# Layer 1 of a two-layer edge-convolution network on one core: GpSimd's two adds of a step ahead of its four gathers

## What is computed

```python
def _edge_conv(x, src, dst, W1, b1, W2, b2):
    x_i = x[dst]
    x_j = x[src]
    h = jnp.concatenate([x_i, x_j - x_i], axis=-1)
    m = _leaky(h @ W1 + b1) @ W2 + b2
    return jax.ops.segment_sum(m, dst, num_segments=N_NODES)

h = jnp.maximum(_layernorm(x, axis=-1), 0.0)
h = _edge_conv(h, src, dst, W1_0, b1_0, W2_0, b2_0)
h = _leaky(_layer_norm(h, ln_g0, ln_b0))
h = _edge_conv(h, src, dst, W1_1, b1_1, W2_1, b2_1)
h = _leaky(_layer_norm(h, ln_g1, ln_b1))
return x + h
```

## Time and profile before

| | |
|---|---|
| median of the runs shown | 1081.89 us |
| lowest and highest of them | 1065.54, 1090.26 us |
| the profiled execution | 1051.49 us, its span 1049.8 us |
| granted TensorE clock, mean | 0.938 |
| PE, DVE, ACT busy | 848.6, 816.5, 591.7 us |
| POOL busy | 727.7 us |
| POOL: gathers of layer 1 | 196, 197.4 us |
| POOL: adds (L597) | 98, 127.3 us |
| DVE: L856 of the form e_n <- e_v | 50, 59.3 us |

### The profile page before, as it was taken

One profiled execution on the slowest core, in us unless ns is written; L12 is line 12 of the kernel. 1 busy time (PEld: TensorE's weight loads), 2 busy tenths in 40 slices (PEclk: granted clock), 3 DMA queues, 4 the chain that ended last, 5 costly groups with the idle time before them and its releaser, 6 DMA issues.

```text
span 1049.8 us, 21951 instructions
## 1 busy us (share of the span) xinstructions
PE 848.6 (81%) x5756; PEld 691.8 (66%) x5756; DVE 816.5 (78%) x2330; ACT 591.7 (56%) x1632; POOL 727.7 (69%) x705
## 2 busy tenths in 40 slices
PE   1577788898889898988998647998888888888864
PEld 1345676777777677766777545777777777777753
DVE  6675687787887788787876313799999999999984
ACT  0145787888888788887888410433434343343431
POOL 4877777777777777777730007788888888888544
PEclk9998899999999999999999855999999999999965
DMA  1232477888687778776875551699999999999996
GB/s 38 77 81 76 109 173 190 210 201 212 182 211 190 203 193 214 193 203 179 199 183 133 145 151 49 149 246 276 272 272 265 270 270 259 276 267 266 256 265 174
DMA packets 338395, 204.11 MB, mean 194 GB/s; under 512 B 32986, under 2 KB 322589, under 8 KB 338269
## 3 DMA queue, kind: packets, MB, share of 16 engines
q1 hardware_dynamic: 190397, 99.95, 38.6%
q10 hardware_dynamic: 129056, 64.16, 22.2%
q0 software_dynamic: 18816, 38.57, 14.2%
HBM read 124.92 MB, written 77.62 MB: 193 GB/s over the span
## 4 chain that ended last, share of the span: by engine, by line
POOL 32%; DVE 23%; issue 21%; PE 8%; DMA 7%; ACT 4%; SPq 3%; DVEq 0%; ACTq 0%; POOLq 0%
POOL e_x L583 18%; POOL e_x L576 14%; DVE e_hT L856 5%; DVE e_n L856 5%; PE psum L902 3%; DVE e_same L750 3%; DMA e_x<-in_x,src_cols 3%; DVE e_rows L866 3%; DVE e_hidT L877 2%; SPq L531 2%; DMA b_rows<-e_rows 2%; DVE w_rel L735 1%; DMA h_rows<-w_out 1%; ACT e_n L633 1%; DVE n_stats L799 1%
## 5 line engine op out<-in xcount | busy, mean ns | idle before, releaser
L583 POOL DMA_INDIRECT e_x<-h_rows,src_cols x196 | 197.4, 1007 | 148.0 <-DMA h_rows<-w_out 93.9
L902 PE MATMUL psum<-w_win,w_oh 113*128 113x128 f32 x1568 | 227.0, 291 | 36.0 <-ACT w_out L613 21.7
L583 POOL DMA_INDIRECT e_x<-in_x,src_cols x196 | 205.9, 1051 | 59.8 <-issue 59.5
L576 POOL DMA_INDIRECT e_x<-in_x,dst_idx x196 | 194.2, 991 | 73.1 <-issue 58.2
L902 PEld LDWEIGHTS psum<-w_win,w_oh 113*128 113x128 f32 x1568 | 206.9, 205 | 42.2 <-issue 31.5
L618 ACT ACTIVATE e_v<-psum 128x512 f32<-128x512 f32 x98 | 59.4, 606 | 218.2 <-DVE e_hT L856 96.7
L910 PE MATMUL psum<-e_same,e_m 128*128 128x136 f32 (+2 forms) x1168 | 169.7, 290 | 0.0
L910 PEld LDWEIGHTS psum<-e_same,e_m 128*128 128x128 f32 x1168 | 149.3, 197 | 23.2 <-issue 21.2
L738 DVE TENSOR_TENSOR w_oh<-node_iota,w_rel 112x512 f32<-112x512 f32 x196 | 142.1, 725 | 6.7
L799 DVE BATCH_NORM_STATS2 n_stats<-e_x 128x6 f32<-128x128 f32 x392 | 80.4, 278 | 70.2 <-DMA e_x<-in_x,src_cols 69.1
L633 ACT ACTIVATE e_n<-e_x,n_shift,n_inv 128x128 f32<-128x128 f32 x196 | 80.5, 490 | 0.7 <-DVE n_shift L833 0.5
(11 more groups left out here) (164 smaller groups left out, 1677.9 us busy)
## 6 DMA issues: line engine op xcount, KB each, us to landing
w_win<-b_rows SPq DMA_DIRECT2D x784, 56.4 KB
h_rows<-w_out SPq DMA_DIRECT2D x98, 256.0 KB
e_line<-dst_lines SPq DMA_DIRECT2D x49, 288.0 KB
b_rows<-e_rows SPq DMA_DIRECT2D x49, 258.0 KB
b_rows<-e_rows ACTq DMA_DIRECT2D x49, 258.0 KB
e_x<-in_x ACTq DMA_DIRECT2D x49, 256.0 KB, 5.0
out<-e_x ACTq DMA_DIRECT2D x49, 256.0 KB
w_out<-in_x ACTq DMA_DIRECT2D x36, 256.0 KB, 4.8
```

The costliest lines, as they stand in the source:

```text
L576: pool.indirect_dma_start(e_x[:, slot, 0, k, :], None, table, bass.IndirectOffsetOnAxis(dst_idx[:, g * K + k:g * K + k + 1], 0)).then_inc( ...
L583: pool.indirect_dma_start(e_x[:, slot, 1, k, :], None, table, bass.IndirectOffsetOnAxis(src_cols[:, g * K + k:g * K + k + 1], 0)).then_inc ...
L902: last = nc.tensor.matmul(b_p[:, j, :], w_oh[0:W + 1, w % RH, j, :], w_win[0:W + 1, w % RW, j, 0:D], start=True, stop=True)
```

## The change

In layer 1 POOL takes the two adds of its step first and its four gathers after them. The waits of each stay with it. Layer 0 and all other engines have the same instructions in the same order.

```diff
             for s in range(-2, STEPS[1] + 1):
-                if active(s + 2):
-                    gather(pool, 1, s + 2)
                 for w in windows(s - R1 - 5):
                     pool.wait_ge(nodes_made, NODE_GROUPS + w + 1)
                     pool.wait_ge(x_in[w % RQ], 16 * uses(w, RQ) + loads_of(w) - 16)
                     pool.tensor_tensor(x_ring[w % RQ], t_ring[w % RT], x_ring[w % RQ], ALU.add).then_inc(nodes_raised, 1)
+                if active(s + 2):
+                    gather(pool, 1, s + 2)
```

## The result

The changed kernel took **1071.37 us** (median of 20 runs, 1056.30 to 1092.76). The kernel before, run beside it, took 1065.6 us (20 runs, 1044.74 to 1090.26). Ratio 1.0177, 95% interval 1.0141 to 1.0213. A ratio here compares only the executions within 1.5% of the fastest of their kernel (6 of the 20 before and 11 of the 20 after), so it need not be that of the medians, which lie 0.5% apart. The profiled execution took 1069.9 us with a span of 1068.2, against 1051.5 and 1049.8: the same ratio.

A forecast was written before the change was run, and what follows sets the result against it. GpSimd was taken to set layer 1's 7.65 us step; an earlier start with 8.21 us steps ends 21 us later, 1051.5 becoming 1072.6 profiled. The same 21 us on the runs' median of 1081.9 gives 1103 us, range 1074 to 1122.

The forecast's parts named there:

- the two locks: Layer 1: GpSimd's adds hold off VectorE's L856 by 1.42 us; VectorE's two-SBUF-input operations delay gathers by 0.2 to 0.3 us.
- The rule for late gathers: A gather starting during a two-SBUF-input VectorE operation is late by that operation's start + 0.57 − the gather's start.
- The start: Step 9 in layer 1: first adds at 687.17 instead of 692.15, beside L877, then holding off L882.
- rival A: Layer 1: L882 gets between the adds, VectorE is caught at L735 and L738; 7.89 us steps, +7 us, 1089; 25 in 100.
- My own pattern: Layer 1: adds hold off L882, three gathers are late, step 8.21 us instead of 7.65, 21 us later; 45 in 100.
- (a): Layer 1 gathers issued later against their use: costed at nothing, since even a landing of 6.0 us leaves 1.9.
- rival B: Layer 1: nothing happens, adds again meet L866 and L856 of the next step; 7.65 us, 1082; 8 in 100.
- (b): Layer 1: gather(s+2) queues behind the adds' wait for L856; costed at nothing, with 0.25 us to spare.
- (c): ACT's output stores issue up to 5 us sooner, SP's queue waits for nothing of POOL in layer 1; costed at nothing.
- the 30.4 us: Whole kernel: median of the three runs shown (1081.9) above the profiled execution (1051.5), carried into the forecast of 1103.
- The chances by size: Whole kernel: 35 in 100 for slower by over 2%, 61 for within 2%, 4 for faster by over 2%.

The follow-up runs named there:

- e5: The kernel before, unchanged, profiled again in another execution: 1047.63 us.
- e3: Changed order, with the first adds (step 9 only) waiting for both node blocks instead of one: 1075.58 us (4 runs), no ratio.
- e1: Changed order, with the first adds waiting once for VectorE's L862 of step 10: 1077.44 us (6 runs), ratio 1.0194.
- e11: Kernel before, with the first adds waiting once for L862 of step 10, repeated on another chip: 1057.24 us (12 runs), ratio 1.0017.
- e6: Kernel before, with the first adds waiting once for VectorE's L862 of step 10: 1045.90 us (10 runs), ratio 0.9928.
- e2: Kernel before, with the first adds waiting once for VectorE's L750 of step 10: 1075.78 us (12 runs), ratio 1.0011.
- e9: Kernel before, with the adds of every step from the fifth waiting for L862 of VectorE's next step: 1075.01 us (6 runs), ratio 1.0193.
- e10: Changed kernel, with the adds of every step from the fifth waiting for L862 of VectorE's next step: 1079.68 us (4 runs), ratio 1.0262.
- e7: Kernel before, with the second add of each step moved from GpSimd to VectorE behind L856: 1060.20 us (12 runs), ratio 1.0046.
- e8: Changed order, with the second add of each step moved from GpSimd to VectorE behind L856: 1060.98 us (12 runs), ratio 1.0071.
- e4: Kernel before, with GpSimd's adds cut to one element per partition: 1055.00 us (10 runs), ratio 0.9900.
- e12: Changed kernel, with GpSimd's adds cut to one element per partition: 1067.35 us (5 runs) beside 1067.43 for the kernel before, no ratio.

## Why the prediction was right or wrong

*The bound and the two locks: right.* GpSimd sets the step, VectorE's wait is the adds' hold-off. The rule for late gathers held in places that it had not been made from: the gather at 869.02 inside L738 of 868.93 should be late by 868.93 + 0.57 − 869.02 = 0.48 and is by 0.50 (1.44 − 0.94); the one at 872.02 inside L856 of 871.66 by 0.21, and is by 0.20. The Trainium skill, "SBUF — State Buffer", section "Who interferes with whom", has it that `tensor_tensor` does not stall GpSimd's descriptor generation; no stretch of the changed kernel has the 7.35 us step that would follow, and a gather of 1.44 against 0.94 speaks against it. But the gather also reads its indexes (`src_cols`) out of SBUF, and what is held off may be that read and not the descriptors: no run here tells the two apart.

*The start: the first step that failed.* I had the first adds at 687.17 beside L877. They began at 688.30, having waited 2.87 us for VectorE. GpSimd was done with its gathers by 685.43 (forecast 687.14), and VectorE's L856 pair stood at 687.53 instead of 685.64, after 0.89 us of waiting for a window at 685.41. The adds so met L856's second half and were held off, and L882 got in between them with 1.05 instead of 2.7. A start that was fixed to some tenths from one execution of another kernel was not to be had: e5 shows the kernel of before itself starting elsewhere, and by the table below L877 of step 9 moves over 25 us with TensorE's clock.

*The place: rival A's, not mine.* "L882 gets in between here too [...], DVE slips past and is caught later in its step, at L735 and L738", given 25 in 100, is what happened, for the reason given there: the first add had itself been held off. That isn't the only way: in e3 it wasn't, and L882 got in all the same. My own pattern is real and closes on itself (e1: 8.20, e5: 8.25), but it was not the one entered.

*The size in rival A: mis-sized.* It had 7.89 us a step, with "gather 1 behind L738 and one gather behind L856: 7.35 + 0.30 + 0.24". Measured: 7.35 + 0.50 + 0.20 = 8.05. I had put 0.30 for the first gather without laying the step out. L735 is held off until 866.86 + 1.82 = 868.68, so L738 starts at 868.93, only 0.09 ahead of the gather, and the rule gives 0.48. From VectorE's side: 6.24 + 1.82 = 8.06, where A had 1.65 of waiting. Hence 13.9 in the steps and not A's 9 − 2; with the 1.9 of the start that is 15.8 at L877 of step 48.

*What was costed at nothing.* The landing (a) was safe in the L735 place (866.34, the last issue's end, to L877 of the group at 872.86: 6.5 us) but not everywhere: 4.0 to 4.7 us in e1, against the 3.6 that the L856 place leaves. "The trace has no landing time for a gather under this load" was wrong: the packet records of the kernel before have the last packet 3.0 to 5.4 us behind the last issue, 4.0 in the median (groups 11 to 46). That spoke against rival B from the start, since its place leaves 3.6. That is why rival B (7.65, nothing happens) was closed to this order; I had looked at the landing in my own place only. The margin (b) played no part in the steady step, ACT's and SP's queues (c) neither.

*The sum.* Mine, +21 on 1051.5, gives 1072.6; the profiled execution took 1069.9, near it by other terms: 1.9 at the start, 13.9 in the steps, 2.6 in the tail, against 21 from 38 steps of 8.21. So that the forecast of 2.0% (1103 on 1081.9) lies next to the measured ratio of 1.0177 is in good part luck: the changed step gives 13.9 us, 1.3%. By the runs, 1103 was too high and 1071.37 lies 2.6 under the range's end. The failed term is the 30.4 us from the profiled execution to the median of three runs: beside the changed kernel the one before has a median of 1065.6, not 1081.9, 14.1 above its profiled execution. Three runs of a kernel that spreads over 45 us don't fix a median. The chances by size (within 2%: 61) fit the ratio of 1.0177, whose interval crosses 1.02.

*Where each profiled execution spent its time.* The 650 to 700 column is TensorE's granted clock just ahead of the first adds, where TensorE was busy for 46 to 50 of the 50 us; the next two are read at L877 (L879 or L881 in kernels with added lines).

| | clock, 650 to 700 | L877 of step 9 at, us | from there to step 48, us |
|---|---|---|---|
| e5, before again | 1.00 | 679.7 | 303.2 |
| e11, before, one wait | 0.97 | 684.2 | 300.9 |
| before | 0.94 | 686.8 | 299.1 |
| e6, before, one wait | 0.74 | 690.5 | 299.0 |
| e2, before, one wait | 0.83 | 692.1 | 320.4 |
| e3, changed, one wait | 0.97 | 688.8 | 313.2 |
| changed | 0.87 | 688.7 | 313.0 |
| e1, changed, one wait | 0.50 | 704.9 | 324.0 |
| e9, before, wait in every step | 0.50 | 703.5 | 315.3 |
| e10, changed, wait in every step | 0.90 | 685.8 | 327.6 |
| e7, before, split | 0.64 | 698.1 | 308.6 |
| e8, changed, split | 0.91 | 686.3 | 308.6 |
| e4, before, tiny adds | 0.97 | 683.9 | 301.1 |
| e12, changed, tiny adds | 0.69 | 697.5 | 292.6 |

The last column goes by place, by waits for gathers (e1, e10) and by single late results (e1, e2), not by that clock. The column before it spreads over 25 us with hardly an add run yet, and goes with the clock; the two executions at 0.50 are the latest.

*Cause.* Shown: the place sets the step (e2, e5), the two orders cost the same where one add forces both into one place (e7, e8), and the changed order doesn't stay in the 7.65 place from a start from which the order of before does (e1, e6), with L877 waiting for gathers (e1, e10). The lowest of 20 runs fits: 1056.3, where before reaches 1044.7. Open: how many executions of either kernel run in which place, since only the profiled ones can be seen. Of the old order three (before, e6, e11) kept 7.65 to 7.67 from the second adds on at the latest and two (e2, e5) had other steps as well; of the changed order two (changed, e3) had 8.06 and one (e1) ended at 8.20. Open too is what the change costs on average: the medians of 20 say 0.5%, the ratio 1.8%, and the table's 13.9 us 1.3%. And open is how much of the spread of all runs is TensorE's clock: in the profiled ones up to 25 us lie ahead of step 9, and its mean over an execution is 0.93 to 0.94 in the fastest runs of before and 0.89 to 0.92 in most of those over 1065 us.

## What to carry to other kernels

Where two engines that share an SBUF interface run in lock step, a change of order changes which instructions meet, and the step follows from that place: lay out the step for each place it can fall into, with every hold-off, and ask of each whether the data still land in time there. Look at more than one execution before building on the phase of one, and compare profiles between two marks inside the stretch, since what happened ahead of it can weigh more than the change. And a reordering that gains nothing in the sum of work can still cost the slack that the best place needs.

## What the runs showed that I had not expected

- A `tensor_scalar` on 112x4 numbers, one input in SBUF, is held off through both adds: 2.04 us instead of 0.22. The Trainium skill, "SBUF — State Buffer", section "Who interferes with whom", lists `tensor_scalar` among those that can take the shared pair; the trace agrees. Its rule that whoever issues first has the pair doesn't fit the steady step: L735 asks at 866.86, during the first add, and the second add passes it.
- One late result (0.91 us at L862, e5) moves the kernel from a step of 8.25 to one of 7.65 for the rest of layer 1.
- A semaphore wait that is met 0.1 us before the adds begin still goes with 0.46 us more for the pair of adds behind it (2.96 against 2.50, e9).
- The last packet of four gathers of 64 KB ended 3.0 to 5.4 us after the last issue in the kernel before (DMA share 0.99 to 1.04 by stretch), and L879 started 4.0 and 4.7 us after it in e1 where it waited for them.
- TensorE's clock in the 50 us ahead of the first adds (1.00 in e5, 0.50 in e1) goes with an L877 of step 9 that is 25 us later in e1 than in e5, more than the change costs.
